# A fused macaron block on one core: the start of attention written in another order, two state updates moved from VectorE to ScalarE and GpSimd, and the last map's bias added by VectorE

## The reference

```python
x = L0_attn_x
x = x + 0.5 * _L0_ffn_ref(_layernorm(x, axis=-1), L0_ffn_qweights, ...)
x = x + _L0_attn_ref(_layernorm(x, axis=-1), L0_attn_Q, L0_attn_K, L0_attn_VO)
x = x + 0.5 * _L0_ffn_ref(_layernorm(x, axis=-1), L0_ffn_qweights, ...)
```

## Time and profile before

| | |
|---|---|
| median of 3 runs | 978.12 us (978.08 to 978.23) |
| the profiled execution | 977.8 us, its span 975.9 us |
| granted clock of TensorE, mean | 0.998 |
| busy: PE, DVE, ACT, POOL | 99%, 87%, 83%, 86% of the span |

### The profile page before, as it was taken

One profiled execution on the slowest core, in us unless ns is written; L12 is line 12 of the kernel. 1 busy time (PEld: TensorE's weight loads), 2 busy tenths in 40 slices (PEclk: granted clock), 3 DMA queues, 4 the chain that ended last, 5 costly groups with the idle time before them and its releaser, 6 DMA issues.

```text
span 975.9 us, 19642 instructions
## 1 busy us (share of the span) xinstructions
PE 963.7 (99%) x6085; PEld 516.7 (53%) x6085; DVE 852.9 (87%) x1733; ACT 809.4 (83%) x1362; POOL 835.7 (86%) x959
## 2 busy tenths in 40 slices
PE   8999899999999999999999999999999999999998
PEld 8786344444444444444444444444444444445777
DVE  7879999999999998999999999999999998986664
ACT  6885789888988898888888888888888888888774
POOL 5774798999998999899989999999999998899552
PEclk9999999999999999999999999999999999999999
DMA  9001322222222222222222222222222222221003
GB/s 239 19 2 43 74 68 60 63 60 61 62 66 66 66 66 66 64 65 59 61 61 59 62 63 66 65 66 66 66 66 63 58 64 60 60 63 29 1 1 88
DMA packets 72146, 59.92 MB, mean 61 GB/s; under 512 B 11312, under 2 KB 70960, under 8 KB 72048
## 3 DMA queue, kind: packets, MB, share of 16 engines
q1 hardware_dynamic: 71536, 58.31, 24.4%
q10 hardware_dynamic: 512, 0.40, 0.2%
HBM read 6.23 MB, written 2.10 MB: 9 GB/s over the span
## 4 chain that ended last, share of the span: by engine, by line
PE 94%; DVE 4%; POOL 1%; issue 0%; ACT 0%; DVEq 0%; POOLq 0%; ACTq 0%
PE ps L1371 12%; PE ps L1363 11%; PE ps L1373 11%; PE ps L1372 11%; PE ps L1364 11%; PE ps L1356 7%; PE ps L1248 4%; PE ps L1347 3%; PE ps L1390 3%; PE ps L1386 3%; PE ps L1387 3%; PE ps L1349 3%; PE ps L1348 3%; PE ps L1277 3%; PE ps L1258 2%; PE ps L1289 1%
## 5 line engine op out<-in xcount | busy, mean ns | idle before, releaser
L523 POOL TENSOR_TENSOR p_lo<-work_b,p_hi 128x1024 f16<-128x1024 f32 x256 | 539.8, 2129 | 47.2 <-ACT p_hi L708 46.5
L1042 DVE TENSOR_REDUCE mcol<-ps 128x2 f16<-128x1024 f32 x256 | 301.4, 1221 | 2.2 <-PE ps L1356 2.1
L703 ACT ACTIVATE work_b<-ps,exp_scale 128x1024 f32<-128x1024 f32 x256 | 271.2, 1110 | 35.8 <-PE ps L1364 35.2
L708 ACT ACTIVATE p_hi<-work_b 128x1024 f16<-128x1024 f32 x256 | 256.0, 1054 | 0.0
L1363 PE MATMUL ps<-head_ops 128*128 128x512 f16 x512 | 194.1, 379 | 2.9 <-DVE mcol L1042 1.5
L1371 PE MATMUL ps<-p_hi,xn_hi 128*128 128x512 f16 x512 | 194.7, 380 | 0.9 <-POOL p_lo L523 0.9
L1372 PE MATMUL ps<-p_hi,xn_lo 128*128 128x512 f16 x512 | 194.0, 379 | 0.0
L1373 PE MATMUL ps<-p_lo,xn_hi 128*128 128x512 f16 x512 | 194.0, 379 | 0.0
L1364 PE MATMUL ps<-head_ops 128*128 128x512 f16 x512 | 194.0, 379 | 0.0
L532 POOL TENSOR_TENSOR x<-x,o_sb 128x512 f32<-128x512 f32 x126 | 159.8, 1268 | 5.3
L1053 DVE STREAM_TRANSPOSE head_ops<-mcol 32x128 f16<-32x128 f16 x512 | 155.3, 303 | 9.2
(11 more groups left out here) (161 smaller groups left out, 1406.7 us busy)
## 6 DMA issues: line engine op xcount, KB each, us to landing
head_ops<-pair_ops SPq DMA_DIRECT2D x512, 64.0 KB, 2.0
head_ops<-pair_ops SPq DMA_DIRECT2D x128, 128.0 KB, 2.4
x<-x_dram SPq DMA_DIRECT2D x8, 256.0 KB, 5.8
out<-x SPq DMA_DIRECT2D x8, 256.0 KB, 2.3
vo_last<-wvo_dram SPq DMA_DIRECT2D x1, 1024.0 KB, 11.9
qk<-wq_dram SPq DMA_DIRECT2D x1, 512.0 KB, 4.1
qk<-wk_dram SPq DMA_DIRECT2D x1, 512.0 KB, 5.7
qw<-qweights_dram SPq DMA_DIRECT2D x1, 256.0 KB, 5.6
```

The source lines that it names most:

```text
L523: pool.tensor_tensor(p_lo[:, k % 2, rows, :], p32[:, k % 2, rows, :], p_hi[:, k % 2, rows, :], ALU.subtract).then_inc(plo_done, 1)
L703: nc.scalar.activation(p32[:, k % 2, 2 * a:2 * a + 2, :], s_ps[a], ACT.Exp, scale=exp_scale[:, 0:1]).then_inc(exp_done, 1)
L708: nc.scalar.activation(p_hi[:, k % 2, 2 * a:2 * a + 2, :], p32[:, k % 2, 2 * a:2 * a + 2, :], ACT.Copy).then_inc(phi_done, 1)
L1042: nc.vector.tensor_reduce(mcol[:, pair % 2, :, t, 0], max_ps[pair == 1][t % 2], AX.X, ALU.max, negate=True).then_inc(max_red, 1)
```

## The change

**At the start of attention.** `step_x` of step 11 (two 128x512 operations on DVE) goes away. ACT copies the two banks, scaled by one half, into `o_sb`, and POOL adds them to x (`copy_half`, `add_half`). The second half of batch 0 is normalised by ACT (`apply_half`) instead of DVE. The vo high parts and the vo low parts move, lin2 of steps 9 and 10 is split around `turn_z` and the transposes, and the written-out part now goes on until head 2, so that `slot(k)` begins with 2. Exponentials and high parts alternate.

**At the end.** The bias row's matmul leaves lin2 of the second pass; DVE adds the bias to hT ahead of it (`add_bias`, eight operations 128x512). The last batch is done in two halves: two tiles each on PE, a 128x256 operation on DVE, and a store of 128 KB, the first on SP's queue and the second on ACT's.

```diff
-        SLOTS = range(1, NH)
+        SLOTS = range(2, NH)
...
+            pool.wait_ge(xhat_v, len(V_IN) + 1)
+            vo_low(0)
+            vo_low(1)
             xn_low(0, 0)
             xn_low(0, 1)
-            vo_low(0)
-            vo_low(1)
+
+            def add_half(c):
+
+                b = B - 2 + c
+                pool.wait_ge(x1_ready, b)
+                pool.wait_ge(half_out, c + 1)
+                rows = x[:, b * TT:(b + 1) * TT, :]
+                pool.tensor_tensor(rows, rows, o_sb[:, c, :, :], ALU.add).then_inc(x1_ready, 1)
...
             gelu(0, STEPS - 3)
+            weight_halves(STEPS - 1)
             gelu(0, STEPS - 2, [0])
+            act.wait_ge(moments_ready, 3)
+            apply_half(0, 1, xat_a)
+            gelu(0, STEPS - 2, [1])
             for h in range(2):
                 halves_turned(0, h, half_of(bank[0][0], h))
-            gelu(0, STEPS - 2, [1])
...
+            def copy_half(c):
+
+                b = B - 2 + c
+                act.wait_ge(lin2_done, at(0, STEPS - 1, c))
+                nc.scalar.activation(o_sb[:, c, :, :].rearrange("p a d -> p (a d)"), bank[0][b], ACT.Identity,
+                                     scale=0.5).then_inc(half_out, 1)
...
+            copy_half(0)
             q_high(1, 1)
+            copy_half(1)
             nc.scalar.activation(exp_warm[:, :], ident[:, 0:1], ACT.Exp)
...
+            step_x(0, STEPS - 4, 1)
             dve.wait_ge(moments_ready, 3)
-            norm_apply(batch_tiles(0))
-            step_x(0, STEPS - 4, 1)
+            norm_apply(half_tiles(0, 0))
             step_x(0, STEPS - 3, 0)
+            z_scaled(0, STEPS - 1)
             for h in range(2):
                 split(0, h, half_of(bank[0][0], h))
...
+            def add_bias(i):
+
+                for c, b in unit_batches(i):
+                    dve.wait_ge(lin1_done, at(1, i, c))
+                    nc.vector.tensor_scalar(hT[:, b, :], hT[:, b, :], bias[:, NL - 1:NL], None,
+                                            ALU.add).then_inc(h_biased, 1)
...
                 z_scaled(1, i - 1)
+                if i >= STEPS - UNITS:
+                    add_bias(i)
             z_scaled(1, STEPS - 2)
             seed(1, STEPS - 1)
+            add_bias(STEPS - 1)
             step(STEPS - 4)
             z_scaled(1, STEPS - 1)
...
+            step_x(1, STEPS - 1, 0)
+            for h in range(2):
+                rows = half_tiles(B - 1, h)
+                dve.wait_ge(end_half, h + 1)
+                nc.vector.scalar_tensor_tensor(x[:, rows, :], half_of(bank[1][2 + h], 0), 0.5, x[:, rows, :], ALU.mult,
+                                               ALU.add).then_inc(x_half, 1)
...
             pair_ready(1)
+            pe.wait_ge(half_out, 2)
+            maxima(1, 0)
...
             lin2(1, STEPS - 3)
+            lin2(1, STEPS - 2, [0])
             turn_z(1, STEPS - 1)
-            lin2(1, STEPS - 2)
-            lin2(1, STEPS - 1)
+            lin2(1, STEPS - 2, [1])
+            lin2(1, STEPS - 1, [0])
```

More of the change, by code:

```diff
@@ L770, in _ @@
             k_high(2, 0)
-            for a in range(2):
-                exps(1, a)
+            exps(1, 0)
+            p_high(1, 0)
             q_high(2, 0)
-            for a in range(2):
-                p_high(1, a)
+            exps(1, 1)
+            y_high(0)
+            p_high(1, 1)
             pair_free(3, 1)
             k_high(3, 1)
-            y_high(0)
-            for k in range(1, NH - 1):
+            for a in range(2):
+                act.wait_ge(plo_done, a + 1)
+                exps(2, a)
+                act.wait_ge(av_half, a + 1)
+                p_high(2, a)
+            act.wait_ge(o_done, 1)
+            y_high(1)
+            q_high(3, 1)
+            for k in range(2, NH - 1):
                 slot(k)
@@ L1025, in _ @@
             step_x(0, STEPS - 2, 0)
-            z_scaled(0, STEPS - 1)
+            step_x(0, STEPS - 2, 1)
             def q_low(pair, buf):
@@ L1133, in _ @@
             row_max(0)
-            step_x(0, STEPS - 1, 0)
-            step_x(0, STEPS - 1, 1)
+            k_low(1, 1)
+            reduce_max(1, 0)
             row_max(1)
-            reduce_max(1, 0)
-            k_low(1, 1)
+            reduce_max(1, 1)
             q_low(1, 1)
-            reduce_max(1, 1)
+            reduce_max(1, 2)
             pair_free(2, 0)
             k_low(2, 0)
-            reduce_max(1, 2)
-            q_low(2, 0)
             reduce_max(1, 3)
             row_max(2)
+            q_low(2, 0)
             reduce_max(2, 0)
+            y_low(0)
             reduce_max(2, 1)
-            y_low(0)
             pair_free(3, 1)
             k_low(3, 1)
+            row_max(3)
+            reduce_max(2, 2)
+            scale_out(0)
+            reduce_max(2, 3)
+            y_low(1)
+            late(1)
+            q_low(3, 1)
             for k in SLOTS:
@@ L1484, in _ @@
             project_q(0)
-            lin2(0, STEPS - 2, [1])
+            turn_z(0, STEPS - 1)
             pair_ready(0)
@@ L1503, in _ @@
                 scores(0, 0, a)
-            pair_ready(1)
-            pe.wait_ge(x1_ready, B)
-            maxima(1, 0)
-            head_ready(1)
-            for a in range(2):
-                pe.wait_ge(exp_done, 1 + a)
-                scores(1, 1, a)
+            project_k(2)
             pe.wait_ge(max_red, 5)
             maxima(1, 1)
-            project_k(2)
+            head_ready(1)
+            pe.wait_ge(exp_done, 1)
+            scores(1, 1, 0)
+            pe.wait_ge(max_red, 6)
+            maxima(1, 2)
+            pe.wait_ge(exp_done, 2)
+            scores(1, 1, 1)
             pe.wait_ge(ql_ready, 2)
@@ L1517, in _ @@
             weigh(0, 0)
-            pe.wait_ge(max_red, 6)
-            maxima(1, 2)
+            pe.wait_ge(max_red, 7)
+            maxima(1, 3)
             project_q(2)
             weigh(0, 1)
-            pe.wait_ge(max_red, 7)
-            maxima(1, 3)
             pe.wait_ge(plo_done, 2)
             weigh(0, 2)
+            pair_ready(2)
+            pe.wait_ge(exp_done, 3)
+            maxima(2, 0)
             weigh(0, 3)
-            pair_ready(2)
-            for a in range(2):
-                pe.wait_ge(exp_done, 3 + a)
-                maxima(2, a)
+            pe.wait_ge(exp_done, 4)
+            maxima(2, 1)
             project_k(3)
+            head_ready(2)
+            pe.wait_ge(max_red, 9)
+            scores(2, 2, 0)
+            pe.wait_ge(yl_ready, 1)
+            pe.wait_ge(plo_done, 3)
+            weigh(1, 0)
+            pe.wait_ge(prep_p, 12)
+            pe.wait_ge(prep_a, 6)
+            outputs(0)
+            pe.wait_ge(max_red, 10)
+            scores(2, 2, 1)
+            pe.wait_ge(exp_done, 5)
+            maxima(2, 2)
+            weigh(1, 1)
+            pe.wait_ge(plo_done, 4)
+            weigh(1, 2)
+            pe.wait_ge(exp_done, 6)
+            maxima(2, 3)
+            weigh(1, 3)
+            project_q(3)
             for k in SLOTS:
```

70 lines of the change are left out of this document (48 added, 22 removed).

## The result

| | before | changed |
|---|---|---|
| median of 5 runs | 978.12 us | 972.41 us (972.32 to 972.90) |
| ratio to before | | 0.9944, interval 0.9933 to 0.9954 |
| the profiled execution | 977.8 us, span 975.9 us | 972.9 us, span 971.1 us |

The kernel became 5.7 us faster; 972.9 was predicted, range 971.3 to 975.0. Of the five executions before, four lie within 977.98 to 978.23 and one took 1108.36 us, for which no trace shows a cause; it stands outside the ratio.

The account below looks back on a forecast made before the run. PE was taken to bound the kernel, with DVE and the store behind its last matmul. Start 3.7 plus end 1.6 (1.72 + 0.27 + 0.2 - 0.6) gave 5.3 us off 977.8; median forecast 972.9 us, range 971.3 to 975.0.

Parts of the forecast that it names:

- The layout: Start of attention: operation times laid along the new order; head 3's scores start at 110.13 us, not 113.90.
- The "6.0" us of waits by starts: Start of attention, old order: PE's five waits, 4.77 us in the rows, counted as 6.0 by matmul starts.
- 0.53 between the halves of head 1's scores: Start of attention: a new PE wait of 0.53 us for reduce_max, as the pair's maxima have one buffer.
- Rival C: Start: ACT's chain behind the last copy is late by 1.28 us; start gains 2.4, time 974.2; chance 0.16.
- Rivals E and F: Body: E, POOL or DVE bind, start's gain lost, 976.5, chance 0.05; F, each head slower, net 985.4, chance 0.03.
- A PE with no idle in 725 us: Attention's body: busy windows read as PE never idle, so PE bounds it; the argument against losing the start's gain.
- a pair by about 0.7: End: two add_bias on DVE stop POOL and delay newton by about 0.7 us, 0.3 to 0.4 each.
- PE loses 0.6: End: at step 11's last turn_z PE waits 0.6 us for the second batch, because newton is late.
- rival B: End: newton has slack enough and PE does not lose the 0.6 us; time 972.2; chance 0.18.
- rival D: End: add_bias costs 0.74 us and stops POOL as long; end gains 0.6, time 973.9; chance 0.08.
- The smaller store: End: the last store, 128 KB, saves 0 to 0.3 us, taken as 0.2, the same on either queue.
- forecast A: Whole kernel: start gains 3.7 us, end 1.6; time 972.9, own range 972.0 to 973.8; chance 0.50.

Follow-up runs that it names:

- e1: Kernel before with only the edits at the start of attention, its end the old one; 974.40 us, ratio 0.9963.
- e2: Kernel before with only the edits at the end, its start the old one; 976.66 us, ratio 0.9980.
- e8: Changed kernel with step 11's state updates back on DVE, no copies or additions, scores of head 0 ahead of pair 1's first maxima; 974.66 us.
- e11: Changed kernel with DVE normalising all four tiles of batch 0, ACT's apply_half gone; 974.02 us.
- e7: Changed kernel with a second, scratch-writing 128x512 tensor_scalar of DVE ahead of every add_bias; 973.14 us.
- e9: Changed kernel with the stores of batches 4, 5 and 6 left out; 971.90 us.
- e4: Changed kernel with the state update of batch 2 ahead of the last z_scaled in DVE's queue; 972.28 us.
- e5: Changed kernel with the last batch computed and stored whole, as one DVE operation and one 256 KB store; 972.54 us.
- e6: Changed kernel with the bias row back on PE and add_bias dropped, the halved last batch kept; 973.85 us.

## Why the prediction was right

**The start, 3.7 predicted, 3.55 in the trace and 3.9 by e1.** The layout held step by step. Less the 0.36 us of shift it said 92.20 for the first `maxima` of pair 1, and the row says 92.56 - 0.36 = 92.20; 95.44 for scores of head 1 against 95.85 - 0.36 = 95.49; 110.13 for head 3 against 110.35. The "6.0" us of waits by starts, which stands beside the layout, is too high: the starts of the five rows and of the matmuls ahead of them give some 5.6 (a matmul follows the one before it after 0.215 us, a 128x128 one after 0.11); the forecast of 3.7 goes by the layout. The wait of 0.2 at the first projection is there too, as a gap in front of 83.48 too short for the profile to name. Two predicted waits came out a little smaller or larger: 0.53 between the halves of head 1's scores is 0.23 (by starts 0.40), and 0.27 at head 2 is 0.33 (by starts 0.49). Rival C, ACT's chain late, did not come: the first exponential starts at 93.96, where 93.68 + 0.36 = 94.04 was laid out. The drain that the Trainium skill ("ScalarE: Activation LUTs", section "What ACT_TABLE_LOAD costs") puts beside the load would, as an estimate from that page's figure, have placed it near 95.4; this trace does not agree, with the load starting 0.01 us behind the copy and the next operation 1.29 later.

**The body, 0 predicted, 0.31 measured.** Rivals E and F fell: no head is slower by the 0.042 us of rival F, and PE shows no idle. "A PE with no idle in 725 us" was too strong a reading: pauses of 0.07 to 0.2 us hide below what the windows show. They sum to 0.28 us before and 0.07 after, 0.2 of the 0.31. The body is 796.58 in e1 and 796.90 in e2, so this comes with the start's edits. The layout could not have given it, and e8 and e11, with a body of 797.21 us, show that it can as well fall 0.3 us on the other side of the kernel before.

**The end, 1.6 predicted, 1.30 in the trace and 1.7 to 2.0 by e2 and e1.** That the sum came near the truth was luck, because terms of it were off in opposite directions. Of the signs that the prediction named for itself, those of the start came, and at the end one that it called wrong did: the last `turn_z` has no wait, and POOL's operations beside `add_bias` last 0.30 to 0.37 us, not 0.5. Term by term:

- The eight bias rows on PE: 1.72 predicted, 1.69 to 1.70 measured.
- DVE's last operation: 0.27 predicted, 0.42 against 0.69 measured.
- "So each add_bias delays the chain by 0.3 to 0.4 us, a pair by about 0.7": a pair delays it by 0.2 to 0.3. The reading of the full stop was right, but the price was not. A POOL operation of 0.2 us that begins inside DVE's operation ends with it, so it loses 0.10 to 0.17 us, not the 0.3 to 0.4 that the prediction took. By the Trainium skill, "SBUF — State Buffer", section "Who interferes with whom", when DVE runs in a two-port mode, whichever of the two engines comes second is blocked for the whole instruction of the first. The POOL rows here agree in that POOL ends just behind DVE's operation.
- "PE loses 0.6" at the last `turn_z`: it loses nothing. The layout had 1.4 us of delay and 0.6 of loss, so 0.8 were free; the delay is 0.53, which leaves 0.27, and e7 found 0.2. This is rival B's case; rival D, with more delay still, fell.
- The smaller store, +0.2 predicted: -0.68 in the profile. The bytes do count (1.8 to 1.9 us alone against 2.3, so 0.4 to 0.5), but the other stores now stand in front. That a faster PE moves the stores together is what the prediction did not ask. Without it the end would bring 0.5 us more by the medians of e9.

So forecast A stands at the start, by its own mechanism. At the end B's mechanism held, and an unforeseen loss of the size of A's took its place: there the number was right and the reason was not.

## What to carry to other kernels

Lay the chain out step by step from the rows of the trace, waits included, and compare starts, not busy times: over 35 us this came out within some 0.2 us. When an engine ends sooner, ask what its results are handed to: here the faster lin2 of the last steps moved the stores together, onto DMA engines that were still full, and a part of what PE won was lost behind them. A short POOL operation that met a DVE tensor_scalar here lost what was left of that one and no more; price such a meeting at 0.10 to 0.17 us, not at DVE's whole operation. And a sum that fits does not show its terms: here two wrong ones at the end cancelled.

## What the runs showed of the hardware

- Five stores issued between 965.11 and 967.75 us in the changed kernel fill the 16 DMA engines at 282 to 290 GB/s from 966 to 970 us; the last two, of 128 KB, land 1.0 to 1.5 us later than they do alone in e9.
- SP's issue at 963.53, of the second of two stores 0.6 us apart, took 1.53 us instead of 0.37. The DMA engines were not full then (0.19 busy from 963 to 964, 0.74 from 964 to 965), and in e9 the same issue took 0.37; what held it stays open.
- TensorE's granted clock falls early in the span in some executions. In the changed kernel's profile PE was busy for 0.92 and 1.00 of the two microseconds from 7 to 9 us, and the clock stood at 0.50 (1.2 GHz) from 9 to 12 us; in e4's it stood there from 8 to 14 us. In e5's, with PE busy for 1.00 of both, it stayed at 1.00 (2.4 GHz). Executions of mean clock 0.996 took 0.7 to 1.3 us more than the others of the same kernel (e1: 975.36 and 975.60 against 974.26 twice and 974.40; e6: 974.56 and 974.61 against 973.80 to 973.85). It is not the whole of the scatter: e8's longest, 976.76, has 0.998. What sets it off isn't known.
- DVE's and POOL's rows lock to each other: POOL ends 0.05 to 0.06 us behind the DVE tensor_scalar in each of the eight meetings in the changed kernel and the sixteen in e7.
